# Seam between causal attention and the second routed FFN: earlier loads, statistics, transposes and table load for FFN group 0

## The reference, cut to what matters

```python
x = x + 0.5 * ffn(_layernorm(x))        # FFN1
x = x + attention(_layernorm(x))        # causal, one head of 128, Wo back to 256
x = x + 0.5 * ffn(_layernorm(x))        # FFN2, same weights as FFN1
```

## Time and profile before

| | |
|---|---|
| median of 3 runs | 1125.11 us (1125.04 to 1126.46) |
| the profiled execution, its own time | 1124.27 us |
| its span, first to last instruction | 1122.4 us |
| PE busy | 998.5 us, 89% |
| DVE busy | 693.8 us, 62% |
| ACT busy | 566.5 us, 50% |
| POOL busy | 492.2 us, 44% |
| mean granted clock of PE | 0.951 of full speed |
| attention, about | 446 to 707 us of the span |
| FFN2 a starts (first U) | 707.03 us |

### The profile page before, as it was taken

One profiled execution on the slowest core, in us unless ns is written; L12 is line 12 of the kernel. 1 busy time (PEld: TensorE's weight loads), 2 busy tenths in 40 slices (PEclk: granted clock), 3 DMA queues, 4 the chain that ended last, 5 costly groups with the idle time before them and its releaser, 6 DMA issues.

```text
span 1122.4 us, 21178 instructions
## 1 busy us (share of the span) xinstructions
PE 998.5 (89%) x7006; PEld 919.9 (82%) x7007; DVE 693.8 (62%) x1732; ACT 566.5 (50%) x1184; POOL 492.2 (44%) x537
## 2 busy tenths in 40 slices
PE   4899997699999999489998996999998489999997
PEld 4788886699899999478887886778887389999997
DVE  4588878645455554466766666578877444555553
ACT  5657656244454443145554554676655145544552
POOL 3145453545566555651221001336444435665665
PEclk9899998679999999699999998999999779999999
DMA  4011143122221121310112113012111212211221
GB/s 152 17 60 57 67 160 113 75 68 59 68 64 56 56 60 55 94 39 11 48 62 62 39 38 125 27 37 97 57 58 57 91 51 75 69 47 56 67 75 39
DMA packets 50802, 73.13 MB, mean 65 GB/s; under 512 B 5150, under 2 KB 43424, under 8 KB 50080
## 3 DMA queue, kind: packets, MB, share of 16 engines
q1 hardware_dynamic: 42016, 45.75, 13.7%
q0 software_dynamic: 8704, 26.29, 6.2%
HBM read 41.54 MB, written 31.00 MB: 65 GB/s over the span
## 4 chain that ended last, share of the span: by engine, by line
PE 66%; DVE 15%; POOL 5%; DMA 5%; issue 5%; ACT 4%; SPq 0%; POOLq 0%; DVEq 0%; ACTq 0%
PE banks4to L395 30%; PE bank L395 23%; PE banks4to L1492 4%; DVE out_rows L920 2%; DMA slot_z<-routed_rows 2%; PE banks4to L357 2%; PE bank L1061 2%; DVE pT_lo L1732 1%; DVE zT_lo L826 1%; PE bank L1504 1%; POOL attn_x L1814 1%; DVE gT_lo L837 1%; PE bank L483 1%; POOL routed_rows L775 1%; PE bank L473 1%
## 5 line engine op out<-in xcount | busy, mean ns | idle before, releaser
L1208 DVE TENSOR_TENSOR relu_squared<-relu 128x512 f32<-128x512 f32 x136 | 158.8, 1184 | 104.9 <-ACT relu L1159 65.3
L1266 POOL TENSOR_TENSOR hr_lo<-relu_squared,hr_hi 128x512 fp32r<-128x512 f32 x136 | 186.9, 1384 | 77.0 <-DVE relu_squared L1208 72.2
L1159 ACT ACTIVATE relu<-bank,slot_k_bias 128x256 f32<-128x256 f32 x204 | 84.9, 467 | 183.6 <-PE bank L395 162.0
L395 PE MATMUL banks4to<-v_hi,hr_hi 128*128 128x256 f32 x544 | 155.7, 286 | 3.3 <-DVE slot_out L1217 2.8
L395 PE MATMUL banks4to<-v_hi,hr_lo 128*128 128x256 f32 x544 | 152.5, 280 | 0.0
L395 PE MATMUL banks4to<-v_lo,hr_hi 128*128 128x256 f32 x544 | 152.5, 280 | 0.0
L775 POOL DMA_INDIRECT routed_rows<-out_rows,row_index x64 | 66.0, 1032 | 152.6 <-DVE row_index L908 138.0
L395 PE MATMUL bank<-shT_hi,k_hi 128*128 128x256 f32 x408 | 118.9, 291 | 7.3 <-issue 5.6
L395 PE MATMUL bank<-shT_hi,k_lo 128*128 128x256 f32 x408 | 117.1, 287 | 0.0
L395 PE MATMUL bank<-shT_lo,k_hi 128*128 128x256 f32 x408 | 116.9, 286 | 0.0
L395 PEld LDWEIGHTS banks4to<-v_hi,hr_hi 128*128 128x128 f32 x544 | 102.4, 188 | 7.3 <-issue 6.9
(11 more groups left out here) (254 smaller groups left out, 2956.7 us busy)
## 6 DMA issues: line engine op xcount, KB each, us to landing
slot_row<-routed_rows SPq DMA_DIRECT2D x34, 258.0 KB
slot_z<-routed_rows SPq DMA_DIRECT2D x34, 256.0 KB
x_rows<-in_x SPq DMA_DIRECT2D x8, 512.0 KB, 4.0
attn_x<-x_after_ffn SPq DMA_DIRECT2D x16, 256.0 KB, 2.8
attn_out<-x_after_ffn SPq DMA_DIRECT2D x16, 256.0 KB, 2.7
x_after_attention<-attn_out SPq DMA_DIRECT2D x16, 256.0 KB, 2.1
x_rows<-x_after_attention SPq DMA_DIRECT2D x8, 512.0 KB, 4.3
raw_k<-in_k_w SPq DMA_DIRECT2D x2, 1024.0 KB
```

Source lines behind the costliest of these rows:

```text
L395: mm = pe.matmul(outv, w(pw), m(pm), start=(n_first and k == 0), stop=(n_last and k == 2))
L1159: last = act.activation(b.r[q % 2][:, (h % 2) * SLOT:(h % 2 + 1) * SLOT], b.bank(1 + q)[:, (h % 2) * SLOT:(h % 2 + 1) * SLOT], ACT.Relu, b ...
L1208: dve.tensor_tensor(b.sq[q % 2][:, :], b.r[q % 2][:, :], b.r[q % 2][:, :], ALU.mult).then_inc(f["sq"], 1)
L1266: pool.tensor_tensor(b.hr[p][1][:, 2 * q:2 * q + 2].rearrange("p h n -> p (h n)"), b.sq[q % 2][:, :], b.hr[p][0][:, 2 * q:2 * q + 2].rearr ...
```

## The change

SP loads x of groups 0 and 1 in its part s = 9 and only groups 2 and 3 in its part s = 12. DVE takes the statistics of groups 0 and 1 one turn sooner each (turns 13 and 14). ACT normalises group 0 at the end of turn 15, behind a new small Sigmoid (128x2) whose result nobody reads. PE transposes z of group 0 in turn 16: one column between the output of block 14 and the weighing of block 15, the other behind that weighing. DVE forms `zT_lo` of group 0 ahead of y(15). PE's wait for y(15) moves from before the first U to before the second.

```diff
-def transpose_z(pe, b, f, g):
+def transpose_z(pe, b, f, g, columns=range(CC)):
...
-    for c in range(CC):
+    for c in columns:
...
@@ ffn_a_tensor, U
+            if a and g == 0 and n == 1:
+                pe.wait_ge(a["y"], NB)
...
         pe.wait_ge(a["olo"], NB)
         pe.wait_ge(a["exp"], chunk_count(NB))
-        pe.wait_ge(a["y"], NB)
...
+def z_lo_first(dve, b, f):
+
+    for c in range(CC):
+        dve.wait_ge(f["zhi"], 1 + c)
+        dve.tensor_tensor(b.zT[0][1][:, c], b.bank(c), b.zT[0][0][:, c].bitcast(F32), ALU.subtract).then_inc(f["zlo"], 1)
...
@@ ffn_a_vector
-    else:
-        lo(0, f["zhi"], b.zT[0], f["zlo"])
...
@@ attention_sync
-        if s == 12:
+        if s == 9:
             sp.wait_ge(a["T"], 2 * QB)
             sp.wait_ge(a["V"], 2 * QB)
+        if s == 12:
             sp.wait_ge(a["S"], chunk_count(12))
-            for g in range(X_BUFS):
-                sp.dma_start(b.x[g][:], xg[g]).then_inc(f["x_in"][g], 16)
+        for g in {9: (0, 1), 12: (2, 3)}.get(s, ()):
+            sp.dma_start(b.x[g][:], xg[g]).then_inc(f["x_in"][g], 16)
...
@@ attention_tensor
-        if s == NB + 1:
-            pe.wait_ge(a["ptlo"], pairs_before(NB))
-            transpose_z(pe, b, f, 0)
         if s >= 2:
             output(s - 2)
+        if s == NB:
+            transpose_z(pe, b, f, 0, (0,))
         weigh_some(s - 1, 0, min(1, half))
+        if s == NB:
+            transpose_z(pe, b, f, 0, (1,))
...
@@ attention_scalar, end of the turn
-        if s == NB:
+        if s == NB - 1:
+            act.activation(b.cmax[:, 0, 0:ST], b.half[:, 0, 0:ST], ACT.Sigmoid)
             normalize(act, b, f, 0, range(GT))
...
@@ attention_vector
+        if s == NB + 1:
+            z_lo_first(dve, b, f)
         if s >= 2:
             y(s - 2)
...
-        if s in (NB - 2, NB - 1):
+        if s in (NB - 3, NB - 2):
             dve.wait_ge(a["z"], 2 * QB)
-            row_stats(dve, b, f, ahead, s - NB + 2)
+            row_stats(dve, b, f, ahead, s - NB + 3)
```

## The result

| | before | changed |
|---|---|---|
| median of 7 runs each | 1125.11 us (1120.71 to 1128.54) | 1120.73 us (1116.63 to 1121.9) |
| ratio, with its 95% interval | | 0.9949 (0.9926 to 0.9973) |
| a second comparison (e0_changed below), 22 and 12 runs | 1124.47 us (1119.97 to 1129.08) | 1118.76 us (1117.04 to 1123.17), ratio 0.9958 (0.994 to 0.9975) |
| the profiled execution, its span | 1122.4 us | 1117.0 us |
| mean granted clock of PE | 0.951 | 0.952 |

The changed kernel is faster by some 0.4 to 0.5%, and 1120.1 us had been predicted. The medians differ by 4.4 us in the first comparison and by 5.7 in the second. The first interval allows 3.0 to 8.3 us, and single runs of the two kernels overlap.

The account below looks back on a forecast made before the run. Bound taken: mostly PE's matmuls, with the late x transfer delaying first U, which sets the end. -5.48 + 0.22 - 1.15 + 1.26 = -5.15, clock +0.2, about -5.0 from 1125.11: 1120.1 us; 8-in-10 range 1118.2 to 1122.3.

Parts of the forecast that it names:

- ACT's block: End of ACT's turn 15: table load, small Sigmoid and four `z_rows` delay `oT_hi` of block 14 by 3.52 us.
- the seam's term: Last exponential to first U: +1.26 us; wrong if that stretch is not near 8.7 us (7.4 before).
- x at part s = 9: SP's part s = 9: the two loads cost 0, landing by about 667 us, their first reader near 680.7.
- Statistics: DVE's turns 14 and 13: the x wait gone, -5.48 us; group 0's statistics one turn sooner, +0.22.
- Last exponential: End of turn 15: ACT's last exponential can start 6.41 us earlier (5.48 - 0.22 + 1.15).
- the clock term in turn 15: Turn 15: without the long wait PE keeps its clock and two DVE waits go, -1.15 us.
- Seam at full clock: Replay of handovers between ACT, DVE and PE up to first U: near 8.7 us, +1.26 against before.
- The clock: Seam and first U: one fall of PE's clock, between the two places, +0.2 us; bounds -1.66 to +2.1.
- Table load with a drain: ACT's table load in its new place: about 1.4 us more beside it, total 1121.5 us; chance 0.04.
- never lost: Seam and first U: PE's clock does not fall, -6.8 us, total 1118.3 us; chance 0.17.
- in both places: PE's clock falls in the seam's sparse work and at U: -3.1 us, total 1122.0 us; chance 0.17.
- slower: Seam into FFN2 a: PE idles, then runs 20 us at low clock, +3.2 us, total 1128.3 us; chance 0.03.

Follow-up runs that it names:

- e0_changed: The changed kernel run again, nothing altered: ratio 0.9958 to the kernel before (0.994 to 0.9975), seam 10.29 us.
- e6: Changed kernel with 24 unread identity transposes in PE's gap ahead of the output of block 14: ratio 0.9956 to before, seam 8.67 us.
- e1: Kernel before with only the two x loads moved to SP's part s = 9: ratio 0.994 to before, seam 7.45 us.
- e2: Changed kernel with x loads and statistics back in their old places: ratio 1.0012 to before, seam 10.29 us.
- e4: Changed kernel without the small Sigmoid, so the table is loaded at the first gate: ratio 0.9931 to before, seam 8.77 us.
- e3: Changed kernel with z of group 0 back at ACT's turn 16, transposes in turn 17, no small Sigmoid: ratio 0.9895 to before, seam 6.02 us.
- e5: Changed kernel with z of group 0 between block 15's two exponentials, small Sigmoid at turn 16's end: 1114.17 us, ratio 0.9909 to before.
- e7: Changed kernel with z of group 0 between block 15's exponentials and no small Sigmoid: ratio 0.9927 to before, seam 5.21 us.

## Why the prediction was right, step by step

The mechanism held: the end of the wait for x pays, ACT's block costs a part of it. By its own signs the seam's term would be wrong if the seam were not near 8.7 us. It is 9.90, but e6 puts all of the excess on the clock, which the forecast counted apart.

- **x at part s = 9, cost 0, wait gone.** Right: DVE's 5.53 us wait is gone, and e1 shows that this alone is the gain. Each load landed 4.0 us after its issue, the first issue at 656.15, and so before the 667 that was estimated by putting one load behind the other.
- **Statistics.** +0.22 was predicted for those of group 0 in turn 13. In e1, which leaves them in their old places, the last exponential ends at 11.46, in the kernels with early statistics at 11.52, so it is 0.06: the idle 1.57 us covered nearly all.
- **Last exponential.** -6.41 predicted, 11.53 - 18.20 = -6.67 measured. The difference is that term and the clock term in turn 15: together 0.2 to 0.3 us too cautious.
- **ACT's block.** 3.52 us predicted; `oT_hi` of block 14 moved from 0.10 us ahead of the end of the last exponential to 3.38 behind it: 3.48. PE's gap was predicted at 3.6 and is 3.59.
- **Seam at full clock.** 7.4 + 1.26 = 8.7 predicted; e6 has 8.67. In e6 the handovers ACT, DVE, PE, ACT, DVE, PE come in the order of the replay.
- **The clock.** One fall between the two places, net +0.2, was taken. It fell once, in the sparse work: +1.2 there (9.90 - 8.67) and -1.54 at U (7.23 - 5.69; 1.66 taken), net -0.3. This is the term that was mis-sized, by half a microsecond, for two reasons. First, the fall began only at the fourth matmul of the output of block 14 and ended ahead of the output of block 15. Second, the price of a whole fall in the sparse work, 2.1 us, was too high. In e0_changed the low clock holds from the first matmul of the output of block 14 on, and costs 10.29 - 8.67 = 1.6. The fourth part of the 2.1, 0.4 us for the second column of transposes, is not on the path: from that column's start to the output of block 15 pass 1.13 us in e0_changed and 1.09 in e6, as ACT's `oT_hi` and DVE's `oT_lo` of block 15 run beside it. Why the clock fell at another place in two profiles with the same gap stays open.
- **The moved wait for y(15)**: 0 predicted; in the changed kernel U's first twelve matmuls run without a gap. Right.
- **Table load with a drain.** The Trainium skill, ScalarE: Activation LUTs, section "What ACT_TABLE_LOAD costs", has about 1380 ns of drain beside the 1283 ns load. In the changed kernel's trace the last exponential's accumulator read ends at 691.78, the load runs from 691.79 to 693.07 and the small Sigmoid starts at 693.09. Nothing stands beside the 1.28 us, in front of it or behind. This trace doesn't agree with the drain, and the rival falls.
- **Sum.** To the first U -5.15 was predicted without the clock in the seam; with it -4.2 and -3.8 were measured. At the transposes of group 1, where the clock's gain in U is in, about -5.0 was predicted, and -5.7 and -5.4 measured, against the one profile of before. The rivals "never lost" and "in both places" did not occur, and "slower" neither: in e2 all other parts without the loads add a net 1.0 us in the one profile, and by its ratio (1.0012) that kernel can't be told from the one before.

## What to carry to other kernels

Ask of each moved piece on its own what stands behind it in its engine's queue: here two moved loads gave all the gain, and work moved "early" on ACT stood in front of a copy on which all others waited. If work is to move early, put it into a wait of its own engine: the same four instructions, moved up by one exponential and parted from the table load, took 4.7 us off the seam. A replay of the seam, with durations and handovers from one profile, was right within 0.1 us at full clock (e6), but the clock had to be bounded apart.

## What the runs showed that I had not expected

- The clock of PE fell in e4 with a gap of only 2.07 us in front of the output of block 14. In the kernel before it was 1.00 in the middle of a gap of 3.20 us (206:208) and still 1.00 behind that gap (window 208:209, PE at work again). In two profiles of the changed kernel it fell inside a gap of 3.58 us once and behind one of 3.59 once. The length of one gap doesn't say if or where the clock is lost. In the four profiles with all gaps of the seam below 1 us (e3, e5, e6, e7) it never was.
- How much the untouched parts vary: the stretch up to the anchor ended between 678.1 and 688.3 us and the stretch behind the seam took between 405.6 and 409.6 us, in profiles of the same instructions. The cause of this stays open.
